# An LSTM with residual: the bias and a quarter of the weights on ScalarE's DMA queue

## What is computed

```python
xW = jnp.einsum('ntd,dk->tnk', x, Wx) + b

def step(carry, xw_t):
    prev_h, prev_c = carry
    a = xw_t + prev_h @ Wh
    i = jax.nn.sigmoid(a[:, :Hdim])
    f = jax.nn.sigmoid(a[:, Hdim:2 * Hdim])
    o = jax.nn.sigmoid(a[:, 2 * Hdim:3 * Hdim])
    g = jnp.tanh(a[:, 3 * Hdim:])
    next_c = f * prev_c + i * g
    next_h = o * jnp.tanh(next_c)
    return ((next_h, next_c), next_h)
_, hs = jax.lax.scan(step, (h0, c0), xW)
return x + jnp.transpose(hs, (1, 0, 2))
```

## Time and profile before

| | us |
|---|---|
| median of 3 runs | 2702.5 (2702.49 to 2703.16) |
| the profiled execution | 2702.73 |
| its span, first to last instruction | 2700.9 |
| TensorE matmuls busy | 2658.9 (98%) |
| TensorE weight loads busy | 1604.4 (59%) |
| VectorE busy | 1440.4 (53%) |
| ScalarE busy | 871.4 (32%) |
| mean granted TensorE clock | 0.998 |

### The profile page before, as it was taken

The page is one execution under the profiler, slowest core; times in us unless marked ns, Lnnn a source line. Parts: engine busy times, 40 slices in busy tenths (PEclk is TensorE's granted clock), DMA queues, the critical chain, the costliest instruction groups (busy, mean ns, idle before and its releaser), DMA issues.

```text
span 2700.9 us, 110488 instructions
## 1 busy us (share of the span) xinstructions
PE 2658.9 (98%) x49154; PEld 1604.4 (59%) x49154; DVE 1440.4 (53%) x4642; ACT 871.4 (32%) x2721; POOL 8.0 (0%) x20
## 2 busy tenths in 40 slices
PE   4999999999999999999999999999999999999998
PEld 1445555666666666666666666666666666666665
DVE  5555555555555555555555555555555555555554
ACT  4333333333333333333333333333333333333332
POOL 1000000000000000000000000000000000000000
PEclk9999999999999999999999999999999999999999
DMA  6101011011010010110100101101101011011000
GB/s 161 29 19 31 18 28 31 16 31 31 16 31 23 23 31 16 31 31 16 31 23 23 31 16 31 31 16 31 26 20 31 18 29 31 16 31 31 16 16 17
DMA packets 141595, 76.19 MB, mean 28 GB/s; under 512 B 8837, under 2 KB 140549, under 8 KB 140549
## 3 DMA queue, kind: packets, MB, share of 16 engines
q1 hardware_dynamic: 140672, 71.60, 10.5%
q0 software_dynamic: 768, 4.20, 0.6%
q10 hardware_dynamic: 132, 0.07, 0.0%
HBM read 42.27 MB, written 33.55 MB: 28 GB/s over the span
## 4 chain that ended last, share of the span: by engine, by line
PE 98%; DMA 1%; SPq 0%; issue 0%; ACT 0%; DVE 0%; ACTq 0%; DVEq 0%
PE gates L178 98%; DMA w_raw<-in_L_cond_Wh_dram 1%; SPq L133 0%; SPq L123 0%; SPq L151 0%; ACT w_hi L269 0%; DVE x_ring L333 0%; ACT i_f L247 0%; ACT tanh_c L254 0%; DVE h_full L317 0%; DVE c_state L311 0%; DVE f_c L307 0%; DVE i_g L309 0%; ACTq L105 0%; DVEq L318 0%
## 5 line engine op out<-in xcount | busy, mean ns | idle before, releaser
L178 PE MATMUL gates<-w_hi,xT 128*32 128x512 f16 x16384 | 1092.5, 380 | 30.0 <-ACT gates L238 30.0
L178 PEld LDWEIGHTS gates<-w_hi,xT 128*32 128x32 f16 x16384 | 553.4, 97 | 363.2 <-ACT gates L238 30.9
L247 ACT ACTIVATE i_f<-gates 128x256 f32<-128x256 f32 x512 | 196.1, 383 | 1523.1 <-PE gates L178 1523.1
L307 DVE TENSOR_TENSOR f_c<-i_f,c_state 128x128 f32<-128x128 f32 x512 | 149.6, 292 | 973.2 <-ACT i_f L247 973.2
L178 PE MATMUL gates<-w_hi,hT_hi 128*32 128x512 f16 x8192 | 545.8, 379 | 3.1 <-ACT w_hi L269 3.1
L178 PE MATMUL gates<-w_lo,hT_hi 128*32 128x512 f16 x8192 | 546.1, 379 | 0.9 <-DVE w_lo L342 0.9
L178 PE MATMUL gates<-w_lo,xT 128*32 128x512 f16 x8192 | 547.0, 380 | 0.0
L178 PE MATMUL gates<-w_hi,hT_lo 128*32 128x512 f16 x8192 | 546.0, 379 | 0.5 <-issue 0.5
L178 PEld LDWEIGHTS gates<-w_lo,hT_hi 128*32 128x32 f16 x8192 | 276.6, 97 | 168.2 <-DVE w_lo L342 3.2
L178 PEld LDWEIGHTS gates<-w_lo,xT 128*32 128x32 f16 x8192 | 277.1, 97 | 166.3 <-issue 1.8
L178 PEld LDWEIGHTS gates<-w_hi,hT_lo 128*32 128x32 f16 x8192 | 276.9, 97 | 165.3 <-issue 0.8
(11 more groups left out here) (21 smaller groups left out, 598.8 us busy)
## 6 DMA issues: line engine op xcount, KB each, us to landing
x_ring<-in_x_dram SPq DMA_DIRECT2D x256, 128.0 KB, 2.9
out_dram<-x_ring SPq DMA_DIRECT2D x252, 128.0 KB, 2.1
w_raw<-in_L_cond_Wx_dram POOLq DMA_DIRECT2D x8, 256.0 KB, 9.9
w_raw<-in_L_cond_Wx_dram SPq DMA_DIRECT2D x8, 256.0 KB, 13.8
w_raw<-in_L_cond_Wh_dram POOLq DMA_DIRECT2D x8, 256.0 KB, 19.3
w_raw<-in_L_cond_Wh_dram SPq DMA_DIRECT2D x8, 256.0 KB, 26.7
out_dram<-x_ring SPq DMA_DIRECT2D x8, 64.0 KB, 1.9
bias_raw<-in_L_cond_b_dram SPq DMA_DIRECT2D x4, 64.0 KB, 23.0
```

The source lines that it names most:

```text
L178: mm = nc.tensor.matmul(gates[bank][j * N:(j + 1) * N, :], stationary, w[:, which, k, j, :], start=False, stop=False, skip_group_check=True)
L247: nc.scalar.activation(i_f[:, :], bank[:, 0:2 * P], ACT.Sigmoid, scale=UNSCALE).then_inc(if_ready, 1)
L307: nc.vector.tensor_tensor(f_c[:, :], i_f[:, P:2 * P], c_state[:, :], ALU.mult)
```

## The change

The four bias DMAs go from SyncE's queue to ScalarE's, behind the load of h0. After them ScalarE issues row block 2 of all eight tiles. SyncE keeps row block 0 of each tile and GpSimd loads row blocks 1 and 3. `w_loaded[n]` is still raised by two DMAs per tile, one of SyncE's and one of ScalarE's, and `w_loaded_pool[n]` by two of GpSimd's, so the waits of `split_hi` stay as they are. SyncE waits for the last tile of weights on both semaphores before it issues x of steps 8 to 31.

```diff
             def load_w(n):
 
-                for j in range(J // 2):
-                    sp.dma_start(w_raw[j * N:(j + 1) * N, n, :], w_v[n][j]).then_inc(w_loaded[n], 16)
+                sp.dma_start(w_raw[0:N, n, :], w_v[n][0]).then_inc(w_loaded[n], 16)
 
             def chunk(c, loads=True):
                 slot, t_out, t_in = c % SLOTS, c * CHUNK, (c + SLOTS) * CHUNK
@@ -146,12 +145,11 @@
             load_x(0, 0)
             for n in range(J):
                 load_w(n)
-            for j in range(J):
-                src = bias.rearrange("(o g f) -> o g f", o=1, g=GATES)[:, :, j * P:(j + 1) * P]
-                sp.dma_start(bias_raw[j * N:(j + 1) * N, :].rearrange("p (g f) -> p g f", g=GATES),
-                             src.broadcast_to([N, GATES, P])).then_inc(bias_loaded, 16)
             for n in range(J, 2 * J):
                 load_w(n)
+
+            sp.wait_ge(w_loaded[2 * J - 1], 16 * (J // 2))
+            sp.wait_ge(w_loaded_pool[2 * J - 1], 16 * (J // 2))
             for c in range(1, SLOTS):
                 sp.wait_ge(x_loaded, c * X_DMA)
                 load_x(c, c * CHUNK)
@@ -167,7 +165,7 @@
         @block.gpsimd
         def _(pool):
             for n in range(2 * J):
-                for j in range(J // 2, J):
+                for j in (1, 3):
                     pool.dma_start(w_raw[j * N:(j + 1) * N, n, :], w_v[n][j]).then_inc(w_loaded_pool[n], 16)
 
         @block.tensor
@@ -270,6 +268,12 @@
                                          scale=WSCALE).then_inc(w_hi_ready, 1)
 
             act.dma_start(h0_raw[:, :], h0.rearrange("n (j f) -> j n f", j=J)).then_inc(h0_loaded, 16)
+            for j in range(J):
+                src = bias.rearrange("(o g f) -> o g f", o=1, g=GATES)[:, :, j * P:(j + 1) * P]
+                act.dma_start(bias_raw[j * N:(j + 1) * N, :].rearrange("p (g f) -> p g f", g=GATES),
+                              src.broadcast_to([N, GATES, P])).then_inc(bias_loaded, 16)
+            for n in range(2 * J):
+                act.dma_start(w_raw[2 * N:3 * N, n, :], w_v[n][2]).then_inc(w_loaded[n], 16)
             act.preload_act_table_set("sigmoid_and_others")
             act.wait_ge(x_loaded, X_DMA)
             cast_x(0)
```

## The result

The change makes the kernel slower: 2708.12 us (median of 16 runs, 2706.41 to 2710.91) against 2703.19 (16 runs, 2701.81 to 2705.92), a ratio of 1.0018 with a 95% interval of 1.0011 to 1.0026. That is 4.9 us. The point forecast was a gain of 2.8 us, the range reached up to 2704.0, and the measured time lies outside it. The profiled execution took 2708.02 us with a span of 2706.2, 5.3 more than the one of before.

A forecast was written before the change was run, and what follows sets the result against it. The prediction took the prologue to be bound by weight transfers, the only part the change could move. Gains of 1.8 us (prologue end) and 1.0 (clock) sum to 2.8 off 2702.5 or so: 2699.8 us, range 2696.4 to 2704.0.

The forecast's parts named there:

- What bounds the kernel: Whole kernel: TensorE busy 98%, 511 steps of some 2,647 us untouched; the change can move only the transfer-bound prologue.
- Step one, the turns: Weight loading from 8.0 us: three queues get a third of the bytes each, 6.69 MB gone by 32.3 us.
- Step one, the rate: Weight loading with three queues: 275 GB/s taken, between bounds of 248 and 288.
- H: Weight transfers: queues writing the same half of the partitions hinder each other; in the prediction a reason for 275, below 288.
- Step two, the tail: End of weight loading: GpSimd's queue alone moves 1.23 MB at 240 GB/s, 5.1 us, to 37.4 us.
- Step three, VectorE as the bound: End of prologue: VectorE's splits from tile 5 on end at 42.6 us instead of 44.4, gain 1.8 us.
- Step four, the clock: TensorE's dense work after the prologue: 1.0 us lost to the halved clock instead of 2.1, gain 1.0 us.
- What costs nothing: ScalarE's 12 extra DMA issues (through at 9.0 to 17.1 us) are covered; SP's wait before x costs next to nothing.
- D: Rival, weight loading: GpSimd's queue is starved, prologue ends at 44.5 to 45.5 us, at worst 2705; chance 0.10.
- E: Rival, prologue: ScalarE hangs in its own DMA issues and starts its splits late, 2708.3 us; chance 0.04.
- T: Time when ScalarE is free of its issues; prologue ends no earlier than 20 us later, decisive from 24 us.
- C: Rival, weight loading: rate hangs on what is read or written, not queue count; no change, 2702.5 us; chance 0.13.

The follow-up runs named there:

- the dose (8, 16, 32 rows): Changed kernel with the bias of one gate, two gates or all four loaded (8, 16, 32 rows per engine): 2702.84, 2703.84, 2708.12 us.
- the rows of x: Changed kernel with the four bias DMAs replaced by DMAs of the same form that read rows of x: 2706.84 us.
- the halves apart: Changed kernel with block 1 on ScalarE's queue and blocks 2 and 3 on GpSimd's: 2707.52 us against 2703.68 for the kernel before, ratio 1.0014.
- Wh mixed: Kernel before with SP loading blocks 0 and 2, GpSimd 1 and 3, for the Wh tiles alone: 2703.98 us against 2704.51, ratio 0.9998.
- the mixed kernel: Kernel before, two queues, with SP loading blocks 0 and 2 and GpSimd 1 and 3 of all tiles: 2703.95 us against 2703.68, ratio 1.0001.

## Why the prediction was wrong

**What bounds the kernel** held: nothing outside the prologue moved (the table's remainder is 2656.2 us before and 2656.4 after), and the 5.3 us are the prologue's.

**Step one, the turns: the step that failed.** It gave three queues a third of the bytes each. A third each is right for packets and wrong for bytes. The bias was priced at its 0.26 MB among 4.46 and taken to make way at once; it took until 27.5 us and held block 2 of every tile behind it. The row was there: in the earlier trace rows SP's queue has 232 packets and 0.17 MB beside GpSimd's 239 packets and 1.32 MB, equal counts and very unequal bytes. I read the MB and not the packets. Forecast for tile 4 was 30.0 us; in the changed kernel ScalarE came to it at 41.21, since it was still at the Wx tiles, of which the first had come at 31.29, where the prediction had 17.7 at the late end. The counts of the queues, the dose (8, 16, 32 rows) and the rows of x show this cause. Of the 9.0 us between the forecast end (42.6) and the measured one (51.6) it makes up 5.7: with 8 of the 32 rows the end is 45.9. The remaining 3.3 us are left when 24 of the rows are gone, and they alone are more than the forecast gain of 1.8: the kernel with a quarter of the bias took 2702.84 us. Tile 4 later than 32.3 was the first sign of being wrong that the prediction named.

The Trainium skill says in "DMA: Bandwidth & Descriptors", section "Queues, rings and completion order", that each DMA engine goes round the queues at packet granularity; the equal counts agree (134, 130, 131 records). The same passage has 9 to 17 descriptors in a typical packet; the bias and the x rows in its place went one row to a turn after 8 us, so the measurement decides for one. I had weighed the round as "shares" and left out its unit.

**Step one, the rate: mis-sized.** 275 GB/s was taken between 248 and 288; the three-queue kernels moved 230 to 249 from 8 to 22 us. Part of it is H, which the prediction mentioned in passing: with mixed halves two queues moved 251 against 265 to 288. Part is open: with only the bias moved, and with the halves apart, the rate was 238 to 244 with two queues and different halves. A third queue at the start seems to leave the engines in an order that doesn't recover; this is argued, not shown. And 288 itself was the best of three profiles. Every run with three queues has small rows beside the weights for a time (with the bias on SP's queue those of x's first chunk, at 249 GB/s), so what a third queue costs by itself is open.

**Step two, the tail,** came out other than built. GpSimd's queue was not alone and not the last: ScalarE's ran beside it and past it (last rows of weights at 41.3 and 43.1 us), and the two moved 225 GB/s. That a queue alone with both halves gives about 240 was right (238 and 239 where it nearly occurs, on SP's queue).

**Step three, VectorE as the bound,** was the right mechanism with the wrong start: from the first tile, not from tile 5. The chain that ended last is ScalarE's and VectorE's splits from 35.9 to 51.6. Four tiles from ScalarE's start on tile 4 were to take 10.6 us; they took 51.64 - 41.21 = 10.4.

**Step four, the clock:** a gain of 1.0 us was forecast, 2.1 came. It was within the bounds given, but by luck: the forecast had the matmuls with x start at 27 us, a fall of the clock at 37.8 and a rise at 44.6. In fact they started at 40.80, the clock rose at 46.6 after an unbroken row of matmuls, and had not fallen again when the dense work began. It is not a property of the change alone: of the kernels with their last wait at 46 us some had the slow stretch and Wh mixed had none.

**What costs nothing.** ScalarE's 12 issues ended at 7.87 and its table load at 9.2, within 9.0 to 17.1, and delayed nothing. The wait of SP for the last weights cost nothing (ratio 1.0001). The bias wait went, but its place was behind a larger one.

**The rivals.** D had the right kind of cause, a queue that starves while the tiles wait for it, but named GpSimd's, with a price of at most 2705. E's cause did not occur, since ScalarE's issues ended at 7.87. But E had the second half of what happened: ScalarE starts late on tile 0 and VectorE then works through all eight tiles in a row, some 20 us, which it said decides from 24 us on. That its 2708.3 us is next to the measured 2708.12 is chance; it rests on a T of 30 us that was only assumed. C's argument was half right after all: the low rate of the tail hung on what was written. The rule of the Trainium skill that stood for it, in "DMA: Bandwidth & Descriptors", section "Rules for kernel authors", that spreading over queues brings no bandwidth, fits the mixed kernel, where one queue nearly alone moved 239 GB/s and two 251; my reading of 207 against 288 as the worth of a second queue was wrong. The loss of 4.9 us lies under the 0.2% that I had called the limit, so "same" held as a class, but the sign was wrong and the range too narrow on that side.

## What to carry to other kernels

Price a queue in turns, not in bytes: count the rows per DMA engine of all that stands ahead of a transfer on its queue, and multiply by the length of a round of the busy queues (here 0.5 to 1 us a row). Small rows belong on a queue with nothing urgent behind them (the bias alone on ScalarE's queue cost nothing); and a tile that is split over queues is only there with the slowest of them. When a queue is left alone, let it write both halves of the partitions by turns (238 or 239 GB/s against 207 to 217). Before a gain of a few microseconds is built on one profile's transfer rate, look at a second profile: here the same code gave 265 to 288 GB/s.

## What was not expected of the hardware

- A row of 512 B beside rows of 8 KB costs a whole turn: 0.5 to 0.6 us of delay per row and engine for what stands behind, where its own share of the engines' time is a few per cent (5.5% for 110 packets).
- x's first chunk is hit too: its cast was at 9.20 to 15.11 us with the bias or its like at the head of ScalarE's queue, but at 19.76 and 20.83 with weights there, behind h0. Up to 8 us small rows pass several to a turn (1077 packets on SP's queue beside 115 of GpSimd's). What ends this is open.
- The rate of full engines varied from 207 to 217 GB/s (one queue, one half of the partitions) over 238 to 251 (one queue or two with mixed halves) to 265 to 288 (two queues, a half each). In the two kernels with a third queue at the start, two queues with a half each moved 238 and 244 later on; why is open.
